# Two graph-attention layers on one core: adjacency loaded by GpSimd's indirect DMA in pieces of 1 MB, edge masks kept with one bit per edge

## The chip, the cores and the metric

The kernel runs on one core of one Trainium2 chip. The metric is the device time of one execution in microseconds. A core has TensorE (PE in the rows; PEld is its weight load), VectorE (DVE), ScalarE (ACT), GpSimd (POOL), the queue engine SyncE (SP), and 16 DMA engines that all queues share.

## What is computed

8192 nodes with 128 features go through two layers of masked attention over the same dense 8192 x 8192 int32 adjacency matrix (268 MB):

```
def layer(x, adj, W, b, a1, a2):
    h  = relu(layernorm(x))
    Wh = h @ W + b
    e  = leaky_relu((Wh @ a1)[:, None] + (Wh @ a2)[None, :], 0.2)   # one score per edge
    p  = softmax(where(adj > 0, e, -9e15), axis=1)
    return x + p @ Wh
x = layer(x, adj, ...)     # layer 0
x = layer(x, adj, ...)     # layer 1, the same adj, other weights
```

## The kernel before

**Scores as signs.** An edge's leaky score is linear in each of its two signs, so the kernel needs for each edge only one bit "edge" and one bit "the score is negative". For each tile of 128 output rows it builds two byte masks, `g1` and `g2`, whose bytes are 0 or one fp8 number, and TensorE multiplies both with prepared node rows (`node_rows`): 128 matmuls for one tile, 64 tiles in a layer. Two `masks` buffers, two `sign_a` and two `sign_z` buffers are used in turn (`T.p` is the tile's parity).

**The stages.** First a node stage computes layer 0's projected rows for 64 node tiles: statistics on VectorE, `rstd` and sums on GpSimd, projection on TensorE, scaled rows on ScalarE, stored to DRAM by SP and loaded back in four quadrants (`load_quadrant`). Then come the 64 tiles of layer 0, then the opening of layer 1, then its 64 tiles.

**Layer 0, tile k.** The bodies of the engines run side by side, each engine in its own written order:
- SP loads 4 MB of adjacency per tile. `adj_sb` has four slots `r` of 1 MB; slot `r` is loaded by four DMAs of 32 partitions x 8 KB (`load_adj`, L248 to L253), and is refilled for the next tile when ScalarE's cast of this tile has read it (`cast_done`, L331). Behind the 16 loads SP stores the finished rows of x, loads x of the next tile and stores the node rows of layer 1.
- ScalarE in body k (L663 to L682): `part_one(k-1)`, at odd k `store_pair`, then cast(k+2, 0), `node_copy(k-2)`, z_sign(k+2, 0), cast(k+2, 1), z_sign(k+2, 1), cast(k+2, 2), `node_high(k-2)`, cast(k+2, 3). A cast turns one adjacency slot to a byte per edge in `sign_a`. `node_high` writes `b_and_d` and then `row_parts`.
- VectorE in body k (L996 to L1039): its two z signs of tile k+1 around the weighing of tile k-1, `mask_bits(k+1)`, `pack(k+1)`, the transpose `turn_bits(k+1)`, `node_ext(k-2)`, the shifts `split_g1` and `split_g2`, and the small steps of tiles k-1 and k-2 between them. `node_low` waits for ScalarE's and GpSimd's `row_parts`.
- `pack` gathers the edge bits of two tiles in the single buffer `pair_a` (1 MB); ScalarE's queue stores it to `mask_dram` after every second tile, and the next even `pack` waits for that store (`pair_stored`, L832).
- GpSimd in body k of layer 1's node work: `node_step(k)` (waits for `var_eps`, which VectorE writes at the end of its body k+1) and `node_rest(k)`, which waits for `ext(k)` and for `b_and_d(k)` of ScalarE's body k+2, and writes half of `row_parts`.
- TensorE in tile k waits for `g_ready(k)` and for the two accumulators of tile k-2. After chunk 8 of 64 it transposes a node tile of layer 1, after chunk 24 it projects it.

**Layer 1.** No adjacency is read: SP loads `pair_a` from `mask_dram` once for two tiles, and VectorE takes each tile's bits from it (`LOW_Z_WORD`, `SHIFT_G1`, `SHIFT_G2` say where the bits lie).

Of the kernel before, what the change touches and what calls it, by code (L numbers as in the profile page):

```python
# [23 lines left out]
NODES = 8192  # L24
# [28 lines left out]
LOW_Z_WORD = [0x10101010, 0x02020202]  # L53
SHIFT_G1 = [0, 3]
SHIFT_G2 = [1, 4]
KEEP_WORD = [0x30303030, 0x06060606]
# [35 lines left out]
def sweep(eng, body, trail=0, step=2, head=HEAD):  # L92

    end = TILES - step
    for k in range(head):
        body(Tile(k))
    with eng.Fori(head // step, end // step) as u:
        for k in range(step):
            body(Tile(k, u, step))
    for k in range(end, TILES + trail):  # L100
        body(Tile(k))


def gat_kernel(nc, x, adj, w_0, b_w_0, a_vec_0, b_a_0, w_1, b_w_1, a_1, out):
# [5 lines left out]
    mask_dram = nc.dram_tensor("mask_bytes", (TILES // 2, 128, NODES), I8, kind="Internal").ap()  # L110
# [4 lines left out]
    with ExitStack() as ctx:  # L115
# [10 lines left out]
        adj_sb = sb("adj_sb", [128, RGROUPS, SPAN], I32)  # L126
        sign_a = sb("sign_a", [128, 2, NODES], I8)
# [119 lines left out]
        def _(sp):  # L247
            def load_adj(T, r):  # L248
                for a in QUAD_ORDER:
                    sp.nop(nofuse=True)  # L250
                    sp.dma_start(adj_sb[QROWS * a:QROWS * (a + 1), r, :],  # L251
                                 adj[ds(T.t * TILE + QROWS * r, QROWS), SPAN * a:SPAN * (a + 1)]) \
                      .then_inc(adj_loaded[r], 16)  # L253

# [48 lines left out]
            adj_after = [BLOCKS, 2 * BLOCKS, 2 * BLOCKS + 3, 3 * BLOCKS]  # L303
            for a in range(QUADS):
                for k in range(BLOCKS * a, BLOCKS * a + NODE_STEP):
# [3 lines left out]
                    if k in adj_after:  # L309
                        load_adj(Tile(0), adj_after.index(k))  # L310
# [11 lines left out]
            def load_pair(T):  # L322
# [3 lines left out]
                sp.dma_start(pair_a[:], mask_dram[ds(T.n, 1), :, :].rearrange("o p c -> p (o c)")).then_inc(pair_loaded, 16)  # L326
# [28 lines left out]
            sp.wait_ge(pair_stored, 16 * TILES // 2)  # L355
# [28 lines left out]
            with sp.Fori(HEAD // 2, TAIL // 2) as u:  # L384
                for k in range(2):
                    layer_1_tile(Tile(k, u))
# [9 lines left out]
        def _(pool):  # L396
# [18 lines left out]
            build_picks()  # L415
            nat_v = nat[:].rearrange("p (c t) -> p c t", c=2)
# [31 lines left out]
            for l in range(LAYERS):  # L448
                if l:
                    pool.wait_ge(S[0].nat_ps, 1)  # L450
                    pool.wait_ge(S[0].coefs, 2)
                    pool.wait_ge(limits, n_limits)

                def body(T):
                    if l and T.u is None and T.k == TILES - 2:
                        pool.wait_ge(S[0].turned, TILES)
                        build_picks()
                    if T.exists:
# [5 lines left out]
                sweep(pool, body, trail=1 - l, step=[NODE_STEP, 2][l])  # L464
# [106 lines left out]
        def _(act):  # L571
# [22 lines left out]
            def cast(T, r):  # L594
# [4 lines left out]
                act.wait_ge(adj_loaded[r], 16 * QUADS * (T.t + 1))  # L599
# [3 lines left out]
            def store_pair(T):  # L603
# [3 lines left out]
                act.dma_start(mask_dram[ds(T.n, 1), :, :].rearrange("o p c -> p (o c)"), pair_a[:]).then_inc(pair_stored, 16)  # L607
# [55 lines left out]
            def layer_0_tile(T):  # L663
# [3 lines left out]
                if T.p == 1 and T.exists and (T.u is not None or T.k < TILES):  # L667
# [16 lines left out]
            sweep(act, layer_0_tile, trail=2)  # L684
# [20 lines left out]
        def _(dve):  # L705
# [107 lines left out]
            def mask_bits(l, T):  # L813
# [4 lines left out]
                else:  # L818
                    dve.wait_ge(pair_loaded, 16 * (T.n + 1))
# [4 lines left out]
                nc.vector.scalar_tensor_tensor(out=bits, in0=bits, scalar=LOW_Z_WORD[T.p], in1=edges,  # L824
# [425 lines left out]
```

## Time and profile before

| | |
|---|---|
| median of 3 runs | 2251.49 us (2243.89 to 2266.31) |
| the profiled execution | 2266.05 us, its span 2264.2 us |
| stages of the span | nodes 0 to 160 us, layer 0 to 1310, opening of layer 1 to 1336, layer 1 to 2264 |
| busy over the span | PE 2015.0 us (89%), PEld 1710.1, DVE 1664.7 (74%), ACT 1134.8 (50%), POOL 347.0 (15%) |
| DMA | 391 MB; 331.62 MB read from HBM, 58.85 MB written |

Busy shares are averages over stages; which engine is late in one of them is read from the waits and the timeline of that stage. A row of the timeline gives start, duration, engine, line and operation, and in brackets the idle time before it with the work that ended it. "SPq" and "ACTq" rows are the issue of a DMA, not its transfer.

### The profile page before, as it was taken

How to read it: one execution, taken by the hardware profiler on the slowest of the kernel's cores; microseconds unless marked ns; L12 is line 12 of the kernel's file. 1: busy time of each engine (PE TensorE's matmuls, PEld its weight loads, DVE VectorE, ACT ScalarE, POOL GpSimd, SP SyncE). 2: the span in 40 equal slices, each digit the busy share in tenths (PEclk: the TensorE clock that was granted, in tenths of full speed). 3: DMA queues.
4: the chain of work that ended last, by engine and by line, in shares of the span. 5: the costliest groups of instructions: out<-in, count | busy, mean ns of one | idle time of the engine just before them, and what ended most of it. 6: DMA issues, size and time to landing. Idle time of an engine off the chain costs nothing.

```text
span 2264.2 us, 49373 instructions
## 1 busy us (share of the span) xinstructions
PE 2015.0 (89%) x16866; PEld 1710.1 (76%) x16866; DVE 1664.7 (74%) x2685; ACT 1134.8 (50%) x1097; POOL 347.0 (15%) x496
## 2 busy tenths in 40 slices
PE   5455889889998898988988979999999999999998
PEld 3234677777777777777877868888888888888887
DVE  6564778778878777787787767777777777777774
ACT  4455667777767676676777433322222223333331
POOL 6440122212222222222222210000000000000000
PEclk9997899999999999999999989999999999999999
DMA  5659999999999999999999681111111111111110
GB/s 145 161 141 243 254 292 280 288 294 309 309 304 269 282 277 278 286 273 288 282 285 296 180 189 47 46 46 46 46 46 46 46 46 46 46 46 46 45 45 11
DMA packets 121683, 390.99 MB, mean 173 GB/s; under 512 B 25137, under 2 KB 74545, under 8 KB 80689
## 3 DMA queue, kind: packets, MB, share of 16 engines
q1 hardware_dynamic: 117040, 357.01, 58.2%
q10 hardware_dynamic: 4608, 33.56, 3.7%
q8 instruction: 18, 0.29, 0.1%
q14 instruction: 17, 0.13, 0.0%
HBM read 331.62 MB, written 58.85 MB: 172 GB/s over the span
## 4 chain that ended last, share of the span: by engine, by line
PE 59%; DMA 25%; DVE 5%; issue 4%; ACT 3%; SPq 2%; DVEq 0%; ACTq 0%; POOL 0%; POOLq 0%
PE acc L538 58%; DMA adj_sb<-in_adj_dram 12%; DMA mask_bytes<-pair_a 11%; DVE masks L845 2%; DMA node_rows<-row_parts 2%; ACT sign_a L600 2%; SPq L251 1%; DVE ext L790 1%; ACT part_a L619 1%; PE ps_h L490 0%; ACT b_and_d L586 0%; ACT row_parts L588 0%; DMA masks<-in_x_dram 0%; DVE row_parts L797 0%; SPq L277 0%
## 5 line engine op out<-in xcount | busy, mean ns | idle before, releaser
L538 PE MATMUL acc<-node_rows,masks 128*128 128x258 f16 x16384 | 1907.9, 278 | 133.7 <-ACT part_a L619 76.0
L538 PEld LDWEIGHTS acc<-node_rows,masks 128*128 128x128 fp8e4 x16384 | 1624.3, 99 | 396.6 <-issue 142.1
L600 ACT ACTIVATE sign_a<-adj_sb 128x2048 int8<-128x2048 int32 x256 | 487.4, 1904 | 142.3 <-DMA adj_sb<-in_adj_dram 137.7
L613 ACT ACTIVATE sign_z<-t_row,neg_s 128x2048 int8<-128x2048 f32 x256 | 503.9, 1994 | 1.0 <-DVE masks L845 1.0
L619 ACT ACTIVATE part_a<-acc,coef_a 128x258 f32<-128x258 f32 x128 | 60.1, 470 | 721.4 <-PE acc L538 721.4
L809 DVE TENSOR_SCALAR sign_z<-t_row,neg_s 128x2048 int8<-128x2048 f32 x256 | 327.0, 1279 | 7.4 <-issue 6.8
L845 DVE STREAM_TRANSPOSE masks<-sign_z 128x2048 uint32<-128x2048 uint32 x128 | 295.0, 2305 | 0.1
L869 DVE SCALAR_TENSOR_TENSOR part_ac<-acc,coef_c,part_a 128x258 f32<-128x258 f32 x128 | 62.1, 485 | 297.8 <-ACT part_a L619 297.6
L435 POOL TENSOR_TENSOR h_sum<-h_sum,ext 128x128 f32<-128x128 f32 x126 | 113.1, 898 | 795.5 <-DVE ext L790 791.8
L833 DVE TENSOR_SCALAR pair_a<-sign_a 128x2048 uint32<-128x2048 uint32 x32 | 39.3, 1227 | 179.8 <-DMA mask_bytes<-pair_a 179.8
L824 DVE SCALAR_TENSOR_TENSOR sign_z<-sign_z,sign_a 128x2048 uint32<-128x2048 uint32 x64 | 146.3, 2285 | 19.7 <-ACT sign_z L613 19.7
L853 DVE TENSOR_SCALAR masks<-masks 128x2048 uint32<-128x2048 uint32 x128 | 155.9, 1218 | 0.1
L860 DVE TENSOR_SCALAR masks<-masks 128x2048 uint32<-128x2048 uint32 x128 | 155.8, 1217 | 0.1
L824 DVE SCALAR_TENSOR_TENSOR sign_z<-sign_z,pair_a 128x2048 uint32<-128x2048 uint32 x64 | 146.3, 2286 | 1.4 <-ACT sign_z L613 1.3
L423 POOL TENSOR_TENSOR rstd<-var_eps,minus_half 128x1 f32<-128x1 f32 x128 | 125.3, 980 | 139.8 <-DVE var_eps L726 139.5
L490 PE MATMUL ps_h<-w_ext,centred_t 128*128 128x133 f32 x256 | 78.0, 397 | 73.1 <-ACT centred_t L575 69.5
L490 PEld LDWEIGHTS ps_h<-w_ext,centred_t 128*128 128x128 f32 x256 | 51.9, 253 | 94.0 <-ACT centred_t L575 71.8
L797 DVE SCALAR_TENSOR_TENSOR row_parts<-ext,b_and_d,row_parts 128x129 f16<-128x129 f32 x256 | 89.0, 349 | 44.6 <-ACT row_parts L588 44.2
L586 ACT ACTIVATE b_and_d<-ext 128x2 f32<-128x2 f32 x128 | 25.6, 200 | 179.3 <-DVE ext L790 132.0
L445 POOL TENSOR_SCALAR row_parts<-ext,b_and_d 128x129 f16<-128x129 f32 x64 | 75.3, 1176 | 17.3 <-ACT b_and_d L586 17.2
L836 DVE SCALAR_TENSOR_TENSOR pair_a<-sign_a,pair_a 128x2048 uint32<-128x2048 uint32 x32 | 73.0, 2282 | 0.0
L485 PE MATMUL ps_t<-ident,centred 128*128 128x128 f32 x128 | 49.4, 388 | 19.6 <-DVE centred L723 18.4
(81 smaller groups left out, 580.2 us busy)
## 6 DMA issues: line engine op xcount, KB each, us to landing
adj_sb<-in_adj_dram SPq DMA_DIRECT2D x1024, 256.0 KB, 10.4
mask_bytes<-pair_a ACTq DMA_DIRECT2D x32, 1024.0 KB, 10.8
pair_a<-mask_bytes SPq DMA_DIRECT2D x32, 1024.0 KB, 4.8
node_rows<-row_parts SPq DMA_DIRECT2D x128, 129.0 KB, 8.1
node_rows<-node_rows SPq DMA_DIRECT2D x32, 516.0 KB, 12.3
x_old<-in_x_dram SPq DMA_DIRECT2D x64, 64.0 KB, 11.9
x_after_layer<-x_new SPq DMA_DIRECT2D x64, 64.0 KB, 12.3
x_old<-x_after_layer SPq DMA_DIRECT2D x64, 64.0 KB, 1.8
```

Source lines behind the costliest of these rows:

```text
L423: pool.tensor_tensor(rstd[:, T.p, :], var_eps[:, T.p, :], minus_half[:], ALU.pow).then_inc(S[l].rstd, 1)
L435: pool.tensor_tensor(h_sum[:], h_sum[:], ext[:, T.p, 0:DIM], ALU.add).then_inc(S[l].h_sum, 1)
L490: pe.matmul(ps_h[:, 0:EXT], centred_t[:, T.p, :], w_ext[l][:], start=True, stop=True).then_inc(S[l].h_raw, 1)
L538: mm = pe.matmul(acc[T.p][s][:, 0:ROW], stationary[s][:, c // BYTES, c % BYTES, :], node_rows[:, c, ROW * s:ROW * (s + 1)], start=(c == 0) ...
L600: nc.scalar.activation(sign_a[:, T.p, SPAN * r:SPAN * (r + 1)], adj_sb[:, r, :], ACT.Sign, scale=-1.0) \
L613: nc.scalar.activation(sign_z[:, T.p, SPAN * r:SPAN * (r + 1)], t_row[:], ACT.Sign, scale=-1.0, bias=neg_s[:, ds(RGROUPS * T.t + r, 1)]).t ...
L797: ins = nc.vector.scalar_tensor_tensor(out=row_parts[:, slot, ROW * s + PART:ROW * (s + 1)], in0=ext[:, T.p, 0:PART], scalar=b_and_d[:, T. ...
L809: nc.vector.tensor_scalar(sign_z[:, T.p, SPAN * r:SPAN * (r + 1)], t_row[:], neg_s[:, ds(RGROUPS * T.t + r, 1)], -1.0, ALU.is_gt, ALU.mult) \
L824: nc.vector.scalar_tensor_tensor(out=bits, in0=bits, scalar=LOW_Z_WORD[T.p], in1=edges, op0=ALU.bitwise_xor, op1=ALU.bitwise_and).then_inc ...
L845: nc.vector.transpose(g2[:, T.p, :].bitcast(U32).rearrange("p (b r i) -> p r b i", r=RGROUPS, i=QROWS), sign_z[:, T.p, :].bitcast(U32).rea ...
L853: nc.vector.tensor_scalar(g1[:, T.p, :].bitcast(U32), words, SHIFT_G1[T.p], EDGE_WORD, ALU.logical_shift_left, ALU.bitwise_and).then_inc(S ...
L860: nc.vector.tensor_scalar(words, words, SHIFT_G2[T.p], EDGE_WORD, ALU.logical_shift_left, ALU.bitwise_and).then_inc(S[l].g_ready, 1)
```

## The change

Three things are changed.

1. The adjacency is loaded by GpSimd. One indirect DMA fills one slot, 128 partitions x 8 KB; partition 32a+i gets columns 2048a to 2048a+2047 of row 128t+32r+i, so one DMA reads 1 MB that is contiguous in DRAM. The row numbers lie in `adj_index` (two sets, each moved on by two tiles after use). Tile 0 is loaded from the fourth step of the first node stage on, tile 1 when its slots are cast, tiles 2 and 3 ahead of layer 1's node work, and then `load_adj(k+4)` stands at the head of GpSimd's body k, ahead of `node_step(k)` and `node_rest(k)`. SP's loads and their place in its order are gone.
2. `pair_a` holds one bit per edge of four tiles. `pack` runs for every tile as before, with other masks (the first of four a tensor_scalar, the other three a scalar_tensor_tensor), the store goes out after every fourth tile, the load in layer 1 comes before every fourth.
3. In layer 1 each tile's bit is doubled in place by VectorE (`double_edges`): one pass ahead of the first of four tiles, two ahead of the last.

```diff
+            def load_adj(T):
+
+                pool.wait_ge(index_ready, QUADS + T.t)
+                for r in range(RGROUPS):
+                    if T.u is not None or T.k:
+                        pool.wait_ge(cast_done, RGROUPS * (T.t - 1) + r + 1)
+                    pool.nop(nofuse=True)
+                    pool.indirect_dma_start(out=adj_sb[:, r, :], out_offset=None, in_=adj_rows_of_2048,
+                                            in_offset=bass.IndirectOffsetOnAxis(ap=adj_index[:, T.p, r:r + 1], axis=0)) \
+                        .then_inc(adj_loaded[r], 16)
+                if T.u is None and T.k == 0:
+                    pool.engine_nop().then_inc(index_ready, 1)
+                else:
+                    pool.tensor_scalar(adj_index[:, 1 - T.p, :], adj_index[:, 1 - T.p, :], float(2 * QUADS * TILE), 1.0,
+                                       ALU.add, ALU.mult).then_inc(index_ready, 1)
...
             for l in range(LAYERS):
                 if l:
+                    load_adj(Tile(1))
                     pool.wait_ge(S[0].nat_ps, 1)
                     pool.wait_ge(S[0].coefs, 2)
                     pool.wait_ge(limits, n_limits)
+                    for k in range(2, LOADS_AHEAD):
+                        load_adj(Tile(k))
...
+                    if l == 0 and T.u is None and T.k == HEAD - 1:
+                        load_adj(Tile(0))
+                    if l and T.plus(LOADS_AHEAD).exists:
+                        load_adj(T.plus(LOADS_AHEAD))
                     if T.exists:
                         node_step(l, T)
                     rest = T.plus(l - 1)
                     if rest.exists:
                         node_rest(l, rest)
...
-                act.wait_ge(adj_loaded[r], 16 * QUADS * (T.t + 1))
+                act.wait_ge(adj_loaded[r], 16 * (T.t + 1))
...
-                if T.p == 1 and T.exists and (T.u is not None or T.k < TILES):
+                if T.p4 == PACK - 1 and (T.u is not None or T.k < TILES):
                     store_pair(T)
...
             def layer_0_tile(T):
-                if T.plus(1).exists:
-                    for r in range(RGROUPS):
-                        sp.wait_ge(cast_done, RGROUPS * T.t + r + 1)
-                        load_adj(T.plus(1), r)
...
-                if T.p == 1 and T.plus(1).exists:
+                if T.p4 == PACK - 1 and T.plus(1).exists:
                     load_pair(T.plus(1))
...
+            def double_edges(T):
+
+                pair = pair_a[:].bitcast(U32)
+                if T.p4 == 0:
+                    dve.wait_ge(pair_loaded, 16 * (T.n4 + 1))
+                    dve.nop(nofuse=True)
+                    nc.vector.scalar_tensor_tensor(out=pair, in0=pair, scalar=1, in1=pair, op0=ALU.logical_shift_right,
+                                                   op1=ALU.bitwise_or).then_inc(edges_ready, 1)
+                if T.p4 == PACK - 1:
+                    dve.wait_ge(S[1].edge_bits, T.t)
+                    nc.vector.tensor_scalar(pair, pair, LAST_BIT_UP, LAST_BIT_WORD, ALU.logical_shift_left, ALU.bitwise_and) \
+                        .then_inc(edges_ready, 1)
+                    dve.wait_ge(edges_ready, 3 * T.n4 + 2)
+                    dve.nop(nofuse=True)
+                    nc.vector.scalar_tensor_tensor(out=pair, in0=pair, scalar=1, in1=pair, op0=ALU.logical_shift_right,
+                                                   op1=ALU.bitwise_or).then_inc(edges_ready, 1)
...
-                if T.p == 0:
+                if T.p4 == 0:
                     if T.u is not None or T.k:
-                        dve.wait_ge(pair_stored, 16 * T.n)
+                        dve.wait_ge(pair_stored, 16 * T.n4)
                     nc.vector.tensor_scalar(pair, edges, KEEP_WORD[0], None, ALU.bitwise_and).then_inc(packed, 1)
```

## Rows read from the trace of the kernel before

**Rows 1.** Windows by stage: length, busy (count) per engine, clock, DMA share, GB/s

```profile
0.00:160.00 160.00, 84.22 (x223) 50.16 (x224) 98.38 (x482) 75.03 (x263) 88.05 (x220) 1.00 0.58 146
160.00:1310.00 1150.00, 1002.07 (x8403) 849.81 (x8401) 874.45 (x1331) 783.92 (x633) 256.36 (x269) 0.94 1.00 277
...
1336.00:2264.00 928.00, 918.40 (x8192) 800.92 (x8192) 674.02 (x832) 262.65 (x187) 0.00 (x0) 0.99 0.14 46
```

**Rows 2.** Waits in 500:1290: engine, line, releaser, us in total, times, longest

```profile
DVE pair_a L833 <- DMA mask_bytes<-pair_a: 141.4, 23, 7.6
...
PE acc L538 <- ACT part_a L619: 76.0, 21, 4.8
...
ACT sign_a L600 <- DMA adj_sb<-in_adj_dram: 30.5, 33, 2.0
```

**Rows 3.** Timelines of ACT, DVE and PE from one mask store on

```profile
912.97 0.34 ACTq L607 DMA_DIRECT2D mask_bytes<-pair_a  x1
...
924.14 1.23 DVE L833 TENSOR_SCALAR pair_a<-sign_a 128x2048 uint32<-128x2048 uint32 x1 [6.60 <-DMA mask_bytes<-pair_a]
...
929.68 1.21 DVE L860 TENSOR_SCALAR masks<-masks 128x2048 uint32<-128x2048 uint32 x1
...
931.14 3.45 PE L538 MATMUL acc<-node_rows,masks 128*128 128x258 f16 x18 [3.86 <-ACT part_a L619]
```

**Rows 4.** The chain that ended last: mask stores of bodies 17 and 61

```profile
495.95 10.21 DMA mask_bytes<-pair_a
...
1260.92 10.38 DMA mask_bytes<-pair_a
```

**Rows 5.** Timelines of PE and ACT: first tiles, tiles 2 and 63 weighed

```profile
176.64 15.84 PE L538 MATMUL acc<-node_rows,masks 128*128 128x258 f16 x128 [12.85 <-DVE masks L860]
206.51 16.24 PE L538 MATMUL acc<-node_rows,masks 128*128 128x258 f16 x128 [14.03 <-DVE masks L860]
...
249.77 0.46 ACT L619 ACTIVATE part_a<-acc,coef_a 128x258 f32<-128x258 f32 x1
...
1309.38 0.47 ACT L619 ACTIVATE part_a<-acc,coef_a 128x258 f32<-128x258 f32 x1 [7.69 <-PE acc L538]
```

**Rows 6.** Timeline of ACT: casts 0 and 2 of body 50, a b_and_d

```profile
907.77 0.20 ACT L586 ACTIVATE b_and_d<-ext 128x2 f32<-128x2 f32 x1
...
913.48 1.91 ACT L600 ACTIVATE sign_a<-adj_sb 128x2048 int8<-128x2048 int32 x1 [0.24 <-issue]
...
921.04 1.90 ACT L600 ACTIVATE sign_a<-adj_sb 128x2048 int8<-128x2048 int32 x1
```

**Rows 7.** Timelines: POOL beside a busy and an idle DVE, and that DVE

```profile
909.23 1.35 POOL L445 TENSOR_SCALAR row_parts<-ext,b_and_d 128x129 f16<-128x129 f32 x1
911.57 1.43 POOL L423 TENSOR_TENSOR rstd<-var_eps,minus_half 128x1 f32<-128x1 f32 x1 [0.98 <-DVE var_eps L726]
...
911.32 1.27 DVE L809 TENSOR_SCALAR sign_z<-t_row,neg_s 128x2048 int8<-128x2048 f32 x1
...
1301.85 0.47 POOL L445 TENSOR_SCALAR row_parts<-ext,b_and_d 128x129 f16<-128x129 f32 x1
...
1307.08 0.55 POOL L423 TENSOR_TENSOR rstd<-var_eps,minus_half 128x1 f32<-128x1 f32 x1
```

**Rows 8.** DMA issues: queue, count, KB each, median us from issue to landing

```profile
adj_sb<-in_adj_dram SPq DMA_DIRECT2D x1024, 256.0 KB, 10.4
mask_bytes<-pair_a ACTq DMA_DIRECT2D x32, 1024.0 KB, 10.8
pair_a<-mask_bytes SPq DMA_DIRECT2D x32, 1024.0 KB, 4.8
```

**Rows 9.** Windows: one pair_a load of layer 1, alone on the DMA engines

```profile
1515.20:1520.00 4.80, 4.80 (x46) 4.18 (x44) 4.80 (x7) 0.00 (x0) 0.00 (x0) 1.00 0.60 218
```

**Rows 10.** Waits in 1336:2264, and the groups of pack and mask_bits

```profile
DVE part_ac L869 <- ACT part_a L619: 244.4, 64, 12.4
...
L833 DVE TENSOR_SCALAR pair_a<-sign_a 128x2048 uint32<-128x2048 uint32 x32 | 39.3, 1227 | 179.8 <-DMA mask_bytes<-pair_a 179.8
L836 DVE SCALAR_TENSOR_TENSOR pair_a<-sign_a,pair_a 128x2048 uint32<-128x2048 uint32 x32 | 73.0, 2282 | 0.0
```

**Rows 11.** Node stage: chain that ended last, and SP's timeline

```profile
22.64 8.20 DMA masks<-in_x_dram
...
91.75 15.59 DMA node_rows<-row_parts
...
87.63 1.82 SPq L251 DMA_DIRECT2D adj_sb<-in_adj_dram  x4
```

**Rows 12.** Timeline of DVE at the opening of layer 1

```profile
1328.92 2.29 DVE L824 SCALAR_TENSOR_TENSOR sign_z<-sign_z,pair_a 128x2048 uint32<-128x2048 uint32 x1 [1.30 <-ACT sign_z L613]
```

More of the change, by code:

```diff
@@ L50 @@
 EDGE_WORD = 0x20202020
[L53 to L56, printed above, removed]
+PACK = 4
+KEEP_WORD = [0x80808080, 0x20202020, 0x08080808, 0x02020202]
+LAST_BIT_UP, LAST_BIT_WORD = 5, 0x40404040
+LOW_Z_WORD = [[0x10101010, 0x02020202] * 2, [0x40404040, 0x10101010, 0x04040404, 0x20202020]]
+LEFT_G1 = [[0, 3] * 2, [-2, 0, 2, -1]]
+LEFT_G2 = [[1, 4] * 2, [-1, 1, 3, 0]]
 VGROUPS = 4
@@ L89, in wait_before, with sweep @@
             eng.wait_ge(sem, self.t - back + 1)
-def sweep(eng, body, trail=0, step=2, head=HEAD):
-    end = TILES - step
+def sweep(eng, body, trail=0, step=2, head=HEAD, tail=None):
+    end = TILES - (tail or step)
     for k in range(head):
@@ L247, in _ @@
         def _(sp):
[L248 to L253, printed above, removed]
             def load_x_old(l, T):
@@ L383, in _ @@
                 layer_1_tile(Tile(k))
-            with sp.Fori(HEAD // 2, TAIL // 2) as u:
-                for k in range(2):
-                    layer_1_tile(Tile(k, u))
+            with sp.Fori(HEAD // PACK, TAIL // PACK) as u:
+                for k in range(PACK):
+                    layer_1_tile(Tile(k, u, PACK))
             for k in range(TAIL, TILES):
@@ L415, in _ @@
             build_picks()
+            pool.iota(adj_index[:].rearrange("p b r -> p (b r)"), pattern=[[QUADS * TILE, 2], [QUADS * QROWS, RGROUPS]], base=0,
+                      channel_multiplier=QUADS).then_inc(index_ready, 1)
+            pool.wait_ge(index_ready, 1)
+            for a in range(1, QUADS):
+                part = adj_index[QROWS * a:QROWS * (a + 1), :, :].rearrange("p b r -> p (b r)")
+                pool.tensor_scalar(part, part, float(a - QUADS * QROWS * a), 1.0, ALU.add, ALU.mult).then_inc(index_ready, 1)
+                pool.wait_ge(index_ready, a + 1)
+            adj_rows_of_2048 = adj.rearrange("n (a c) -> (n a) c", a=QUADS)
+            def load_adj(T):
[12 more added lines that the diff above has]
+                                       ALU.add, ALU.mult).then_inc(index_ready, 1)
             nat_v = nat[:].rearrange("p (c t) -> p c t", c=2)
@@ L462, in body @@
                         node_rest(l, rest)
-                sweep(pool, body, trail=1 - l, step=[NODE_STEP, 2][l])
+                sweep(pool, body, trail=1 - l, step=[NODE_STEP, 2][l], tail=[NODE_STEP, LOADS_AHEAD][l])
         @block.tensor
@@ L682, in layer_0_tile @@
                     cast(ahead, 3)
-            sweep(act, layer_0_tile, trail=2)
+            sweep(act, layer_0_tile, trail=2, step=PACK)
             open_layer(1)
@@ L835, in pack @@
                     dve.wait_ge(packed, T.t)
-                    nc.vector.scalar_tensor_tensor(out=pair, in0=edges, scalar=KEEP_WORD[1], in1=pair,
+                    nc.vector.scalar_tensor_tensor(out=pair, in0=edges, scalar=KEEP_WORD[T.p4], in1=pair,
                                                    op0=ALU.bitwise_and, op1=ALU.bitwise_or).then_inc(packed, 1)
@@ L847, in turn_bits, with to_edge_bit @@
                   .then_inc(S[l].turned, 1)
+            def to_edge_bit(out, words, left):
+                shift = ALU.logical_shift_left if left >= 0 else ALU.logical_shift_right
+                return nc.vector.tensor_scalar(out, words, abs(left), EDGE_WORD, shift, ALU.bitwise_and)
             def split_g1(l, T):
@@ L1008, in tile @@
                     if ahead.exists:
+                        if l:
+                            double_edges(ahead)
                         mask_bits(l, ahead)
@@ L1043, in _ @@
                     choose_path()
-                sweep(dve, tile, trail=2 - l)
+                sweep(dve, tile, trail=2 - l, step=PACK)
         fast_path.close()
```

29 lines of the change are left out of this document (13 added, 16 removed).

## The prediction

> **What bounds the kernel now.** I read the windows by stage first: layer 0 takes 1150 of 2264 us, with the DMA engines busy all the time (share 1.00) at 277 GB/s, while layer 1 is TensorE alone (918.40 us busy of 928) with DMA at 0.14 [rows 1]. So the change can win only in layer 0 and the node stage ahead of it. Then the waits of layer 0's steady part, where the largest on the path is VectorE's even `pack` waiting for the mask store, 141.4 us in 23 times, and TensorE's that follow from it, 76.0 us in 21; ScalarE's casts hardly wait for the adjacency, 30.5 us [rows 2]. The timeline shows the loop that this makes. The store is issued at 912.97 and landed when `pack` starts at 924.14; transpose and shifts end at 930.89, and TensorE starts its tile at 931.14 after 3.86 us of idling, its first 18 matmuls in 3.45 us, 192 ns each where layer 1 takes 918.40/8192 = 112 ns [rows 1, 3]. With the tile's end comes the next store. 22 such rounds of two tiles fill 495.95 to 1260.92, so a tile costs 17.39 us [rows 4], where TensorE needs 128 x 0.112 = 14.35 us and some 0.3 for the node matmuls: 14.65. The first tiles are worse: tile 1 starts at 206.51, 14.03 us late for its masks, and tile 2 is weighed at 249.77 [rows 5]. From there to the weighing of tile 63 at 1309.38 are 61 tiles of 17.37 us.
>
> **The mask store every fourth tile.** The wait of 6.60 us [rows 3] comes half as often. If nothing else were late, four tiles would cost 4 x 14.65 + 3.86 + 18 x 0.08 = 63.9 us, 16.0 a tile.
>
> **The loads' rate.** A 1 MB load over 128 partitions keeps the engines busy 0.60 x 4.80 = 2.88 us, which is 364 GB/s [rows 9]; the 32-partition loads fill them at 277 [rows 1]. The Trainium skill, page "SBUF — State Buffer", section "Door 1: The DMA port swizzle", says that 32 partitions reach 8 of 16 ports and only 128 reach all; the two rates agree with its direction. A tile moves 4.19 MB of adjacency, 0.26 of masks, 0.26 of x and node rows, together 4.7: 13.0 us at 364 GB/s, 17.0 at 277. I take the first, since these loads have its shape; the second is a rival.
>
> **Where the loads are issued, and what they wait for.** This is where I expect the gain to be spent. SP could refill a slot as soon as its cast was done. GpSimd's body k starts with the loads of tile k+4, but it comes there only after `node_rest(k-1)`, which waits for `b_and_d(k-1)`; ScalarE writes that in body k+1, behind casts 0, 1 and 2 of tile k+3. So slots 0 to 2 stand empty until then, and slot 0 is needed again at the head of ScalarE's next body. A ring is closed once per tile, and its length is a sum:
> - from cast 0 to the end of cast 2, with the copy and both z signs: 921.04 + 1.90 - 913.48 = 9.4 us; then `b_and_d`, 0.2 us [rows 6];
> - GpSimd's `row_parts`: 0.47 us beside an idle VectorE, 1.35 beside a busy one [rows 7]. VectorE's `node_low` waits for this very operation in this ring, so I take 0.5;
> - writing the descriptors of one indirect DMA: no row has it. From below SP's issues, 1.82/4 = 0.45 us [rows 11]; from above GpSimd's worst stretching: `rstd` takes 0.55 us alone and 1.43 when it meets VectorE's 1.27 us tensor_scalar, which it sits out [rows 7], so 1 us of work behind two z signs would be 3.5 us. It stands right ahead of z sign 2 of the next body: one meeting, 1.6 us taken;
> - landing: 4.8 us on a quiet queue, 10.8 for a 1 MB transfer among others [rows 8]. Four loads follow one another and need 3 x 2.9 us behind the first, so the queue is nearly empty when the next ring comes round: 4.8 taken.
>
> Sum 9.4 + 0.2 + 0.5 + 1.6 + 4.8 = 16.5 us. In every fourth body the mask store leaves just as load 0 does and shares the engines with it, 2.9 us at most: 0.4 a tile on average. 16.9 us. VectorE's own wait for that store then lies beside the ring: the store lands some 9 us after issue, and `ext` comes about when ScalarE reaches `b_and_d` anyway.
>
> So a tile would cost 16.9 where it cost 17.37, and TensorE would idle about 2 us in each tile, at chunk 24, because its projection waits for `node_copy`, which follows cast 0. The ring is above the 16.0 us of the store alone, so 16.9 is the period.
>
> **The start of layer 0.** Tile 0 starts when it did (176.64) and tile 1 right behind it, at 192.5: the loads of tile 1 go out as tile 0 is cast, ahead of that point as before, and arrive 1 MB every 2.9 us, and tiles 2 and 3 are loaded ahead of the node work. Tile 2 is weighed at 192.5 + 2 x 15.5 = 223.5, 26 us earlier than at 249.77 [rows 5]. Then 59 tiles of 16.9 and two without loads at 14.9 give 1250.4 for tile 63, against 1309.38: 59 us gained, 26 of them before the steady part and 33 in it.
>
> **The rest.** Node stage: row stores wait up to 15.59 us behind quadrant and adjacency loads on SP's ring [rows 11]; 1 MB less in three of these is 3 x 2.9, about 9 us gained. Against that, 4 MB of adjacency now go out early, beside the x loads, for which VectorE already waits 8.20 us [rows 11]: up to 4.19/0.364 = 11.5 us, 7 taken, and 4 x 1.6 us of descriptors on a GpSimd that is in the step's loop. Together 4 us lost (9 gained to 18 lost). Opening of layer 1: one more pass of 2.28 us on VectorE, of which 1.30 fits in its wait [rows 12], 1 us. Layer 1: VectorE's waits are 244.4/64 = 3.8 us a tile, and the added passes are 2.28 us for one tile of four and 1.23 + 2.28 = 3.5 for another [rows 10]. They fit, with 0.3 us to spare; without that cover the second would cost at most 16 x 1 us. 1 us taken. The pack's third and fourth pass of 2.28 where one was 1.23 add 0.26 us a tile to a VectorE that is not the ring. The pair loads halve.
>
> Sum: 2266.05 - 59 + 4 + 1 + 1 = 2213 us for the profiled execution; scaled to the median of the runs (2251.49/2266.05) 2199, say 2200.
>
> **The rivals.**
> - *The loads are fast enough* (descriptors and landing together under 5.5 us). Then the mask store's 16.0 us is the period. For it: the quiet-queue 4.8 us contains an issue already. Against: GpSimd's instructions are 2.6 to 2.9 times as long beside VectorE. 53 us less than my forecast: 2147.
> - *No more bandwidth.* The indirect loads get 277 GB/s; 17.0 us of transfers a tile, the queue never drains, load 0 lands behind the last ones, about 17.7 us. For it: the reads come from the same DRAM rows, and the layer-1 load had the chip to itself. 59 x 0.8 = 47 us more: 2247, no difference.
> - *GpSimd is starved* (slower). While VectorE runs its passes GpSimd writes no descriptors. If each of the four waits for one or two passes, issue takes 3.5 us and load 0 lands at 5.5, `row_parts` back at 1.35: 9.4 + 0.2 + 1.35 + 3.5 + 5.5 + 0.4 = 20.4 us a tile, 59 x 3.5 = 206 more: 2405. The gain is gone from a period of 17.9 us on, which is descriptors and landing at 7.4 instead of 6.4 us, so a milder form of it, 18.4 us, already ends at 2288. The Trainium skill states this mechanism outright: page "SBUF — State Buffer", section "Summary: rules for kernel authors", advises the hardware queues because descriptor writing starves while VectorE is in its faster modes. The rows support the stretching of GpSimd's arithmetic [rows 7]; no run so far shows a descriptor.
>
> **How the numbers follow.** Chances: my ring 0.45, fast loads 0.20, no more bandwidth 0.15, starved 0.20 (most of it mild). A measurement of this kernel tells 1% from no change, 22 us. Faster by over 1%: 0.45 x 0.85 + 0.20 + 0.15 x 0.3 = 0.63; slower by over 1%: 0.16 of the starved and 0.03 of the third; 0.18 between. The range runs from 2125 (below the fast loads, with the node stage's best end) to 2300 (mild starvation).
>
> **What would show it.** Right: casts waiting for `adj_sb` some 4 to 5 us once per tile (250 us and more over layer 0, where its steady part had 30.5), nearly all at cast 0; TensorE idling at the projection for ScalarE's copy rather than at the tile's head; `pack` waiting in only 15 places; tile 2 weighed near 224; layer 1 at 918 us. Wrong: cast 0 not waiting (the order of GpSimd's body costs nothing), GpSimd's DMA instructions far from 1 to 2 us, a DMA share still at 1.00 in layer 0, or a node stage that is longer by more than 20 us.

## The result, and the profile after

The change made the kernel slower by 0.9%: 2271.29 us median of 11 runs (2267.00 to 2274.79) against 2247.78 us of 11 (2236.70 to 2266.31), a ratio of 1.0092 [1.0066, 1.0118]. The forecast was 2200.

| us | before | after | forecast |
|---|---|---|---|
| profiled execution | 2266.05 | 2267.00 | 2213 |
| tile 2 of layer 0 weighed | 249.77 | 222.61 | 223.5 |
| a tile of the steady part (tiles 2 to 60) | 17.43 | 17.92 | 16.9 |
| tile 63 weighed | 1309.38 | 1308.21 | 1250.4 |
| from there to the end of the span | 954.8 | 956.9 | 956.8 |

The head start of 27 us was won, and 59 tiles at half a microsecond more each took it away again. The page of the changed kernel, its busy line and the row of the casts:

```profile
PE 2016.6 (89%) x16866; PEld 1708.1 (75%) x16866; DVE 1778.2 (79%) x2733; ACT 1123.6 (50%) x1097; POOL 762.0 (34%) x819
...
L622 ACT ACTIVATE sign_a<-adj_sb 128x2048 int8<-128x2048 int32 x256 | 486.1, 1900 | 305.0 <-DMA adj_sb<-in_adj_dram,adj_index 300.7
```

The windows by stage, for comparison with [rows 1]:

```profile
0.00:160.00 160.00, 85.15 (x226) 50.69 (x227) 98.08 (x482) 75.43 (x263) 96.71 (x233) 1.00 0.55 150
160.00:1310.00 1150.00, 1002.09 (x8402) 849.15 (x8401) 898.02 (x1334) 772.34 (x633) 662.74 (x580) 0.95 0.71 262
1336.00:2264.00 928.00, 919.70 (x8188) 799.57 (x8186) 761.89 (x873) 261.25 (x187) 0.00 (x0) 0.99 0.09 28
```

TensorE does the same in the same 1150 us of layer 0, but the DMA engines that were full (share 1.00) are now free for 29% of it, while 262 GB/s went through where 277 did. So the traffic as a whole moves at 262/0.71 = 369 GB/s of busy time: the engines have time left, and the loads are issued too late. The same stretch of waits as in [rows 2] says where:

```profile
ACT sign_a L622 <- DMA adj_sb<-in_adj_dram,adj_index: 220.6, 45, 7.8
POOL row_parts L460 <- ACT b_and_d L608: 155.4, 44, 5.1
DVE row_parts L819 <- ACT row_parts L610: 109.0, 43, 4.1
PE ps_h L512 <- ACT centred_t L597: 97.4, 40, 5.5
```

ScalarE waits for the adjacency once per tile, 4.9 us, where all its waits of that kind were 30.5 us; GpSimd waits once per tile for ScalarE; TensorE stops at its projection, not at the head of a tile. The wait of `pack` for the mask store is nearly gone (141.4 us before). The four together are one ring, and two turns of it can be read off the timelines. ScalarE from cast 0 of one body on (start, duration, idle time before with its releaser):

```profile
911.78 1.91 ACT L622 ACTIVATE sign_a<-adj_sb 128x2048 int8<-128x2048 int32 x1 [5.55 <-DMA adj_sb<-in_adj_dram,adj_index]
...
919.34 1.90 ACT L622 ACTIVATE sign_a<-adj_sb 128x2048 int8<-128x2048 int32 x1
921.14 0.19 ACT L608 ACTIVATE b_and_d<-ext 128x2 f32<-128x2 f32 x1
...
928.74 1.91 ACT L622 ACTIVATE sign_a<-adj_sb 128x2048 int8<-128x2048 int32 x1 [3.68 <-DMA adj_sb<-in_adj_dram,adj_index]
...
938.11 0.20 ACT L608 ACTIVATE b_and_d<-ext 128x2 f32<-128x2 f32 x1
...
940.47 0.34 ACTq L629 DMA_DIRECT2D mask_bytes<-pair_a  x1
947.91 1.91 ACT L622 ACTIVATE sign_a<-adj_sb 128x2048 int8<-128x2048 int32 x1 [7.01 <-DMA adj_sb<-in_adj_dram,adj_index]
```

GpSimd beside it:

```profile
921.53 0.38 POOL L460 TENSOR_SCALAR row_parts<-ext,b_and_d 128x129 f16<-128x129 f32 x1 [4.37 <-ACT b_and_d L608]
922.65 1.41 POOL L422 DMA_INDIRECT adj_sb<-in_adj_dram,adj_index  x1 [0.73 <-issue]
924.37 0.94 POOL L422 DMA_INDIRECT adj_sb<-in_adj_dram,adj_index  x1 [0.31 <-issue]
...
938.56 0.38 POOL L460 TENSOR_SCALAR row_parts<-ext,b_and_d 128x129 f16<-128x129 f32 x1 [2.51 <-ACT b_and_d L608]
939.44 1.59 POOL L422 DMA_INDIRECT adj_sb<-in_adj_dram,adj_index  x1 [0.50 <-issue]
...
943.14 3.61 POOL L422 DMA_INDIRECT adj_sb<-in_adj_dram,adj_index  x1 [0.30 <-issue]
```

First turn: cast 0 at 911.78, cast 2 done at 921.24, `row_parts` 921.53 to 921.91, first descriptors written at 922.65 + 1.41 = 924.06, landed 4.68 later at 928.74: 16.96 us. Second turn: descriptors done at 941.03, but the mask store left at 940.47 and the load lands 6.88 us later: 19.17 us. The mean of 36 turns between 500 and 1200 us, beside the forecast's terms:

| term, us | forecast | measured |
|---|---|---|
| cast 0 to `b_and_d`, which starts 0.1 before the end of cast 2 | 9.4 | 9.38 |
| start of `b_and_d` to the start of `row_parts` | 0.2 | 0.42 |
| `row_parts` | 0.5 | 0.38 |
| end of `row_parts` to the first indirect DMA | not counted | 0.62 |
| its descriptors | 1.6 | 1.57 |
| end of descriptors to cast 0 | 4.8 | 4.97 in the three bodies without a store |
| mask store, shared over four | 0.4 | 0.52 (7.04 in the body with the store) |
| sum | 16.9 | 17.86 |

The ring was found, but taken 0.96 us too short; over 59 tiles that is 57 us of the 57.8 by which tile 63 came later than forecast. What the store does in the ring is seen in the packets of the trace: the first packet of load 0 moves 0.70 us after the end of its descriptors in the bodies without a store, and 3.40 us after it in the nine bodies with one, about when the store's last packets end (0.56 us before, on average). So load 0 stands behind the store more than it shares the engines with it.

TensorE's stop of 4.18 us at the projection is followed by a lower granted clock. PE's timeline, then windows of the same stretch (the clock is the third number from the end), and VectorE's `pack` of that body:

```profile
950.02 0.49 PE L512 MATMUL ps_h<-w_ext,centred_t 128*128 128x133 f32 x2 [4.18 <-ACT centred_t L597]
950.36 12.54 PE L560 MATMUL acc<-node_rows,masks 128*128 128x258 f16 x96
```

```profile
946.00:950.00 4.00, 0.00 (x0) 0.00 (x0) 3.18 (x4) 2.09 (x3) 2.45 (x4) 1.00 1.01 428
950.00:951.50 1.50, 1.48 (x10) 1.22 (x11) 0.94 (x3) 1.50 (x1) 0.42 (x1) 0.78 1.00 426
951.50:953.00 1.50, 1.50 (x9) 1.05 (x8) 1.50 (x3) 1.50 (x2) 1.07 (x2) 0.50 1.04 437
953.00:955.00 2.00, 2.00 (x14) 1.53 (x13) 0.86 (x2) 2.00 (x2) 0.00 (x0) 0.68 0.92 365
955.00:963.00 8.00, 8.00 (x74) 7.00 (x73) 3.50 (x8) 5.14 (x6) 3.99 (x4) 1.00 0.29 87
```

```profile
945.40 1.23 DVE L872 TENSOR_SCALAR pair_a<-sign_a 128x2048 uint32<-128x2048 uint32 x1 [0.22 <-DMA mask_bytes<-pair_a]
```

0.50 is the 1.2 GHz level. The 96 matmuls took 12.54 us; at layer 1's 919.70/8188 = 0.112 us each they take 10.8. No term of the ring above has TensorE in it, and ScalarE reached `b_and_d` in these turns without waiting for `ext`, so the slower matmuls lie beside the ring here. The last row says that the mask store had landed by 945.40; by the packets of the trace, what the DMA engines move from 946 to 953 are the queued indirect loads alone (428, 426 and 437 GB/s).

### The profile page after: what moved, and what is told of

Same layout as the page of the kernel before. It is cut to its first block, busy times and chain, and to the rows that moved or that the text cites. A ratio compares the mean times of both kernels' runs of the same rounds, so it can differ in the third digit from the quotient of the medians.

```text
span 2265.1 us, 46517 instructions
## 1 busy us (share of the span) xinstructions
PE 2016.6 (89%) x16866; PEld 1708.1 (75%) x16866; DVE 1778.2 (79%) x2733; ACT 1123.6 (50%) x1097; POOL 762.0 (34%) x819
## 4 chain that ended last, share of the span: by engine, by line
PE 47%; DMA 19%; ACT 14%; issue 14%; DVE 3%; POOL 1%; POOLq 0%; SPq 0%; DVEq 0%; ACTq 0%
PE acc L560 46%; DMA adj_sb<-in_adj_dram,adj_index 17%; ACT sign_a L622 8%; ACT sign_z L635 4%; DMA node_rows<-row_parts 2%; POOL adj_sb L422 1%; DMA masks<-in_x_dram 1%; ACT centred_t L597 1%; DVE ext L812 1%; PE ps_h L512 1%; PE acc L529 0%; ACT b_and_d L608 0%; DVE sign_z L846 0%; DVE masks L884 0%; ACT row_parts L610 0%
## 5 line engine op out<-in xcount | busy, mean ns | idle before, releaser
L422 POOL DMA_INDIRECT adj_sb<-in_adj_dram,adj_index x256 | 447.3, 1747 | 121.6 <-issue 94.6
L512 PE MATMUL ps_h<-w_ext,centred_t 128*128 128x133 f32 x256 | 85.8, 430 | 180.1 <-ACT centred_t L597 172.7
L875 DVE SCALAR_TENSOR_TENSOR pair_a<-sign_a,pair_a 128x2048 uint32<-128x2048 uint32 x48 | 109.5, 2282 | 0.0
L460 POOL TENSOR_SCALAR row_parts<-ext,b_and_d 128x129 f16<-128x129 f32 x64 | 26.4, 412 | 211.4 <-ACT b_and_d L608 211.4
L438 POOL TENSOR_TENSOR rstd<-var_eps,minus_half 128x1 f32<-128x1 f32 x128 | 92.8, 726 | 10.1 <-DVE var_eps L748 4.8
L812 DVE SCALAR_TENSOR_TENSOR ext<-ps_h,rstd,bias 128x133 f32<-128x133 f32 x128 | 43.0, 336 | 36.5 <-PE ps_h L512 35.8
## 6 DMA issues: line engine op xcount, KB each, us to landing
node_rows<-node_rows SPq DMA_DIRECT2D x32, 516.0 KB, 11.7
```

What stands on the lines that cost most here:

```text
L422: pool.indirect_dma_start(out=adj_sb[:, r, :], out_offset=None, in_=adj_rows_of_2048, in_offset=bass.IndirectOffsetOnAxis(ap=adj_index[:, ...
L438: pool.tensor_tensor(rstd[:, T.p, :], var_eps[:, T.p, :], minus_half[:], ALU.pow).then_inc(S[l].rstd, 1)
L512: pe.matmul(ps_h[:, 0:EXT], centred_t[:, T.p, :], w_ext[l][:], start=True, stop=True).then_inc(S[l].h_raw, 1)
L875: nc.vector.scalar_tensor_tensor(out=pair, in0=edges, scalar=KEEP_WORD[T.p4], in1=pair, op0=ALU.bitwise_and, op1=ALU.bitwise_or).then_inc( ...
```

## The experiments

Ten kernels, each an edit of the changed one unless said. The period is that of tiles 2 to 60. Each ratio is to the kernel before on the same chip, whose median there lay between 2247.78 and 2255.42, so ratios are compared, and medians only for large steps. The periods and rows are those of one profiled execution each; that of e3 is the fastest of its four (2188.19 of 2188.19 to 2223.25), so its median belongs to a longer period than the one shown.

| run | what | median | ratio to before [95%] | period |
|---|---|---|---|---|
| changed kernel | | 2271.29 | 1.0092 [1.0066, 1.0118] | 17.92 |
| e1 | loads spread over GpSimd's body | 2165.58 | 0.9628 [0.9588, 0.9668] | 16.09 |
| e3 | packing alone, SP loads | 2211.91 | 0.9849 [0.9786, 0.9912] | 16.19 |
| e4 | loads alone, two tiles per byte | 2300.35 | 1.0223 [1.0181, 1.0266] | 18.35 |
| e5 | store a little earlier | 2264.53 | 1.0055 [1.0033, 1.0076] | 17.88 |
| e6 | ring lengthened | 2312.03 | 1.0238 [1.0156, 1.0321] | 18.56 |
| e7 | `b_and_d` earlier | 2243.00 | 0.9951 [0.9913, 0.9990] | 17.57 |
| e8 | `row_parts` ahead of the sums, loads spread | 2130.96 | 0.9442 [0.9357, 0.9527] | 15.52 |
| e9 | e8 with two tiles per byte | 2196.99 | 0.9728 [0.9649, 0.9808] | 16.60 |
| e10 | e8 with the store earlier | 2077.09 | 0.9216 [0.9193, 0.9239] | 14.65 |
| e11 | store earlier still | 2247.75 | 0.9954 [0.9927, 0.9981] | 17.61 |

**e1: is it the order of GpSimd's body?** Only the places of the four loads move; each of them, with its `cast_done` wait, stays.

```diff
             def node_rest(l, T):
+                ahead = T.plus(LOADS_AHEAD + 1)
+                if l and ahead.exists:
+                    load_adj(ahead, (0,))
                 pool.wait_ge(S[l].ext, T.t + 1)
...
+                if ahead.exists:
+                    load_adj(ahead, (1, 2))
                 pool.wait_ge(S[l].b_and_d, T.t + 1)
...
                                    ALU.mult, ALU.mult).then_inc(S[l].high_d, 1)
+                if ahead.exists:
+                    load_adj(ahead, (3,))
```

> The changed kernel with GpSimd's order alone altered: the load of slot 0 of tile k+5 ahead of node_rest(k), slots 1 and 2 ahead of its wait for b_and_d, slot 3 behind row_parts. Ring theory: slots are refilled as they are cast, as on SP before; the ring of 17.9 us per tile is opened and the period falls to 16.0 us or a little above (mask store every fourth tile, TensorE's 14.65 otherwise): about 110 us less than the changed kernel, near 2160. Rival, descriptors starved or DMA rate the limit: order is without effect, 2270. A further rival, GpSimd now holds up h_sum and rstd behind loads that wait for casts: between 2200 and 2270.

Measured: 2165.58 us, period 16.09, 106 us below the changed kernel with the same loads, bytes and passes. Windows and waits of 500:1100:

```profile
500.00:1100.00 600.00, 558.48 (x4883) 474.44 (x4881) 520.85 (x783) 463.75 (x376) 393.51 (x338) 1.00 0.78 293
```

```profile
POOL h_sum L456 <- DVE ext L822: 168.1, 37, 6.7
DVE row_parts L829 <- POOL row_parts L468: 78.3, 38, 3.2
...
ACT sign_a L632 <- DMA adj_sb<-in_adj_dram,adj_index: 21.1, 15, 2.4
```

The casts wait 21.1 us where they waited 175.0 in this stretch. So the ring through `b_and_d` set the period. In its place VectorE now waits for GpSimd's `row_parts`, 2.1 us in 38 tiles: the sums and the loads of slots 1 and 2 stand ahead of it.

**e3 and e4: the two halves alone.** e3 keeps the four-tile masks and puts SP's loads back; e4 keeps GpSimd's loads and packs two tiles.

```diff
+            def load_adj(T, r):
+                for a in QUAD_ORDER:
+                    sp.nop(nofuse=True)
+                    sp.dma_start(adj_sb[QROWS * a:QROWS * (a + 1), r, :],
+                                 adj[ds(T.t * TILE + QROWS * r, QROWS), SPAN * a:SPAN * (a + 1)]) \
+                      .then_inc(adj_loaded[r], 16)
...
             def layer_0_tile(T):
+                if T.plus(1).exists:
+                    for r in range(RGROUPS):
+                        sp.wait_ge(cast_done, RGROUPS * T.t + r + 1)
+                        load_adj(T.plus(1), r)
```

```diff
-KEEP_WORD = [0x80808080, 0x20202020, 0x08080808, 0x02020202]
+KEEP_WORD = [0x30303030, 0x06060606]
...
-                if T.p4 == PACK - 1 and (T.u is not None or T.k < TILES):
+                if T.p == 1 and T.exists and (T.u is not None or T.k < TILES):
                     store_pair(T)
...
-            def double_edges(T):
```

> One half of the change: four tiles per byte, the adjacency loaded by SP as before. If the store's wait was the period before (17.4 us), it falls to 16.0 to 16.7 us a tile, 40 to 70 us less: 2180 to 2210. Rival, the DMA engines at share 1.00 were the limit as well: 0.26 MB of 5 MB less a tile, 0.9 us at most, 17.0 or more: 2225 or above, as the store's wait turns into casts that wait for adj_sb.

> The other half: adjacency by GpSimd, two tiles per byte as before. Ring theory: the ring of 17.3 us stays, and load 0 shares the engines with a mask store in every second body instead of every fourth (2.1 us each time): 18.4 us a tile, 30 us more than the changed kernel: 2300. Rival, the mask store does not matter to the loads: 2270.

Measured: 2211.91 and 2300.35 us. Packing alone gains 1.5%, the loads alone cost 2.2%, and the two nearly add up to the 0.9% of both. e3's median came out just above what was expected for it and below its rival's 2225. Windows and waits of 500:1100 in its fastest execution:

```profile
500.00:1100.00 600.00, 553.64 (x4842) 476.67 (x4840) 510.31 (x772) 454.98 (x370) 141.03 (x148) 0.99 1.03 291
```

```profile
ACT sign_a L605 <- DMA adj_sb<-in_adj_dram: 111.9, 83, 2.7
DVE pair_a L855 <- DMA mask_bytes<-pair_a: 48.7, 10, 6.3
```

With fewer store waits the 32-partition loads become late themselves: 83 short waits of the casts at a DMA share of 1.03 and 291 GB/s. By that rate a tile's 4.7 MB take 16.2 us, the period of this execution (an estimate from these rows), so loads of this shape leave little below it. In e4 the store falls on the ring every second tile; from its issue to cast 0:

```profile
815.48 0.34 ACTq L626 DMA_DIRECT2D mask_bytes<-pair_a  x1
822.95 1.91 ACT L619 ACTIVATE sign_a<-adj_sb 128x2048 int8<-128x2048 int32 x1 [7.06 <-DMA adj_sb<-in_adj_dram,adj_index]
```

Bodies with a store take 19.3 us there and the others 17.35, so the store costs the ring 2 us each time. One store less in four tiles is 0.5 us a tile or some 30 us in 59 tiles, which covers what packing still buys in the changed kernel: 2300 to 2271.

**e5 and e11: the store off the ring.** e5 issues it in the body before, behind `node_high`; e11 behind cast 1 of that body.

```diff
-                if T.p4 == PACK - 1 and (T.u is not None or T.k < TILES):
-                    store_pair(T)
...
                     cast(ahead, 1)
+                if T.p4 == PACK - 2 and (T.u is not None or T.k < TILES):
+                    store_pair(T.plus(1))
+                if ahead.exists:
                     z_sign(0, ahead, 1)
                     cast(ahead, 2)
```

> The changed kernel with the mask store issued 2.3 us earlier, ahead of cast 3 of the body before instead of behind part_one. Ring theory: load 0 of that tile (8.6 us from issue to cast against 6.5) loses most of its delay, 1 to 2 us in four tiles, 15 to 30 us in all: 2240 to 2255. Rival, the longer landing in the fourth tile comes from elsewhere (the even pack, descriptors held up): 2270.

> The changed kernel with the mask store issued behind cast 1 of the body before, when the loads of that body have mostly landed, so that it has landed before load 0 of the next tile is issued. Ring theory with a term for sharing: load 0 of the fourth tile falls from 8.6 to 6.5 us, four tiles by 2.1 us, 31 us in all: near 2240. Rival, that body's longer landing comes from something else in it: above 2260.

e5: 2264.53, missed; by its timeline the issue of the store began only 1.0 us, and ended 0.6 us, ahead of load 0's descriptors, and load 0 still took 8.34 us from issue to cast, so it told nothing on its own. e11: 2247.75, near what was expected; in its fourth bodies that time is 7.11 us, where it was 8.64, and 6.59 to 6.75 in the others. The store's term is worth 23.5 us by the medians (0.31 x 59 = 18 by the period, 0.0138 x 2250 = 31 by the ratios), of at most 0.52 x 59 = 31.

**e6: the same ring, lengthened on purpose.** Two GpSimd additions of 0.5 us ahead of the loads of every tile.

```diff
+                for k in range(2):
+                    pool.tensor_tensor(scratch[:], ident[:], ident[:], ALU.add).then_inc(index_ready, 1)
+                    pool.wait_ge(index_ready, QUADS + 3 * T.t + k + 1)
```

> The changed kernel with two additions of 128x128 on GpSimd (0.55 us each alone) ahead of the first load of every tile. Ring theory: they lie between row_parts and the descriptors of load 0, so each of some 59 periods is longer by what they take, 1.1 us alone and up to 2.6 beside VectorE: 65 to 150 us more, 2335 to 2420. Rival, the period is set by DMA bandwidth or by VectorE, with GpSimd idle for two thirds of the time: 2270 as before.

Measured: 2312.03, +41 us by the medians (33 by the ratios), the period +0.64. The sign is the theory's and the case without a ring is out, but the size is below what the theory expected. GpSimd's timeline shows the additions in place:

```profile
836.53 0.38 POOL L464 TENSOR_SCALAR row_parts<-ext,b_and_d 128x129 f16<-128x129 f32 x1 [4.77 <-ACT b_and_d L612]
836.87 1.01 POOL L420 TENSOR_TENSOR scratch<-ident 128x128 f32<-128x128 f32 x2
838.77 1.40 POOL L426 DMA_INDIRECT adj_sb<-in_adj_dram,adj_index  x1 [0.89 <-ACT sign_a L626]
```

From `row_parts` to the first load it is now 1.83 us, 1.21 more; the descriptors of load 0 take 1.77 us where they took 1.57, and the landing is shorter, 4.72 us on average where it was 5.49. 1.21 + 0.20 - 0.77 is the 0.64. A later load meets less of the store: the landing falls from 7.04 to 5.23 us in the bodies with one. It also falls from 4.97 to 4.56 us in the others, and why is open. So landing was no constant of the ring, and the expectation, which held it fixed, came out too large.

**e7: `b_and_d` one cast earlier.** Its `node_high` goes behind cast 1, which takes 3.9 us (a z sign and a cast) out of the ring.

```diff
                     cast(ahead, 1)
-                    z_sign(0, ahead, 1)
-                    cast(ahead, 2)
                 if before.exists:
                     node_high(1, before)
                 if ahead.exists:
+                    z_sign(0, ahead, 1)
+                    cast(ahead, 2)
+                if ahead.exists:
                     cast(ahead, 3)
```

> The changed kernel with ScalarE's node_high behind cast 1 instead of behind cast 2; GpSimd's order stays. Ring theory: a z sign and a cast, 3.7 us, leave the ring of 17.9 us, and another limit takes over (about 16.1, as in the interleaved version): about 2165 to 2180. Rival, what the interleaved version gained came from issuing the loads spread out in time rather than from the ring: 2250 or above.

Measured: 2243.00, a third of the gain expected, and below the 2250 of the rival. GpSimd now stands behind `ext` instead (164.7 us in 500:1100, 66.4 before the edit), and works beside a busy VectorE. GpSimd's rows, then two of VectorE in the same turn:

```profile
817.29 1.34 POOL L450 TENSOR_TENSOR h_sum<-h_sum,ext 128x128 f32<-128x128 f32 x1 [2.53 <-DVE ext L813]
818.57 0.25 POOL L451 COPY nat<-ext 128x2 f32 x1
818.81 1.35 POOL L460 TENSOR_SCALAR row_parts<-ext,b_and_d 128x129 f16<-128x129 f32 x1
820.33 1.95 POOL L422 DMA_INDIRECT adj_sb<-in_adj_dram,adj_index  x1 [0.17 <-issue]
```

```profile
807.97 0.49 DVE L912 SCALAR_TENSOR_TENSOR part_ac<-acc,coef_c,part_a 128x258 f32<-128x258 f32 x1 [1.42 <-ACT part_a L641]
...
816.80 0.32 DVE L813 SCALAR_TENSOR_TENSOR ext<-ps_h,rstd,bias 128x133 f32<-128x133 f32 x1
```

So right behind the first path lay a second, whose end is `ext`, `h_sum`, `row_parts`, load 0, with `h_sum` and `row_parts` at 1.35 us each. It does not come straight from the projection: none of the 34 `ext` of this stretch waits for it (it had ended 1.6 to 8.7 us before). `ext` is late by VectorE's own order, in which a z sign, `mask_bits`, `pack` and the transpose stand ahead of it. The last thing that VectorE had waited for (by over 0.3 us) before an `ext` was ScalarE's `part_a`, hence the end of a tile on TensorE, in 25 tiles, and the mask store in the other 9 (47.6 us). TensorE's slower matmuls after a stop can therefore lie on this path, though they lay beside the first. The forecast had not listed it.

**e8 and e9: both rings opened.** Loads 0 and 1 ahead of the wait for `ext`, then `row_parts`, load 2, the sums, load 3; e9 is the same with two tiles per byte, as in e4.

```diff
             def node_rest(l, T):
-                pool.wait_ge(S[l].ext, T.t + 1)
+                ahead = T.plus(LOADS_AHEAD + 1)
+                if l and ahead.exists:
+                    load_adj(ahead, (0, 1))
+                pool.wait_ge(S[l].ext, T.t + 1)
...
+                if ahead.exists:
+                    load_adj(ahead, (2,))
+                keep_sums(l, T)
+                if ahead.exists:
+                    load_adj(ahead, (3,))
```

> The interleaved version with GpSimd's row_parts moved ahead of the sums and behind loads 0 and 1 (there VectorE waited 2.04 us a tile for it, with h_sum and two DMA issues in front of it). If that wait is the period's 1.4 us over TensorE's 14.65, the period falls from 16.1 to about 14.9: some 65 us less, near 2100. Rival, the next limit is close behind (DMA at 0.78 busy, landing of load 1 behind the mask store): 2130 to 2165.

> The version before this one with two tiles per byte as in the kernel before. If the mask store only mattered through DMA engines that the 32-partition loads kept full, the packing is now worth next to nothing (0.26 MB a tile, 0.7 us of DMA time that is free, against 0.26 us of VectorE): within 15 us of it. Rival, each store holds up a load by 2 us and the tile with it, in every second tile instead of every fourth: 20 to 30 us slower.

Measured: 2130.96 and 2196.99, both above what was expected: e8 lies at the edge of its rival's range, though with the mask store's wait and not a late load behind it, and e9 lies outside both of its cases. Waits of e8 in 500:1100:

```profile
DVE pair_a L887 <- DMA mask_bytes<-pair_a: 48.3, 9, 5.6
...
PE acc L575 <- ACT part_a L656: 23.7, 9, 2.9
```

The casts no longer wait, and the store's wait of the kernel before has become the bound again, in half as many places; e9 has it twice as often (90.0 us in 17). With the loads' ring out of the way the packing is worth 66 us, where in the changed kernel it is worth 29.

**e10: and the store earlier.** e8 with the store issued one body ahead, in front of `node_high`.

```diff
                     cast(ahead, 2)
+                if T.p4 == PACK - 2 and (T.u is not None or T.k < TILES):
+                    store_pair(T.plus(1))
                 if before.exists:
                     node_high(1, before)
```

> The version with loads interleaved and row_parts first (2131), and the mask store issued ahead of node_high in the body before, as soon as its pack is done. There every fourth even pack waits 5.3 us for a store that lands after 10 us; the store now goes out some 6 us earlier. If that wait is what is left over TensorE's 14.65 us, four tiles fall from 62.1 to about 59 us and layer 0 by 45 us: near 2088. Rival, DMA engines at 0.84 busy: the early store holds up the loads instead and casts wait for them, 2115 or above.

Measured: 2077.09 us, 7.8% below the kernel before. Windows and waits of 500:1100:

```profile
500.00:1100.00 600.00, 600.00 (x5367) 525.61 (x5365) 576.22 (x859) 489.29 (x404) 473.00 (x363) 1.00 0.87 315
```

```profile
ACT part_a L656 <- PE acc L575: 94.9, 41, 2.6
```

TensorE is busy for all 600 us, a tile takes 14.65 us, the figure worked out for TensorE alone, and the other engines wait for it. All three parts of the change are in this kernel; only places in two orders differ. The same early store with SP's loads was not tried.

## Why the prediction was wrong

- *The sign was wrong because a sum was too small.* The step that failed is the sum of the ring, 16.9 us; it came to 17.86. The gap of 0.62 us between `row_parts` and the first indirect DMA had no term, `b_and_d` was taken at its own 0.2 us though its result is used 0.42 us after its start, and the landing came to 5.49 us on average where 5.2 (4.8 + 0.4) was taken: 0.62 + 0.22 + 0.29, less 0.12, 0.03 and 0.02 for `row_parts`, the descriptors and the casts, is 0.96. The margin against the old period was only 0.5 us a tile, and 1.0 with the 26 us of the start; the two uncounted hand-overs add 0.84. I took point values for 7 us of issue and landing of which no row existed, and the "4.8" from a transfer that was alone on its queue. "Shares the engines" was not it either: load 0 stands behind the store, 2.07 us in every fourth body, 0.52 a tile where 0.4 was taken.
- *The mechanism was right.* e1 takes the ring away and gains 106 us, e6 lengthens it and loses 33 to 41, e4 has it without the new packing at 2300. Casts wait some 4.9 us once per tile, TensorE stops at the projection, `pack` hardly waits, tile 2 is weighed at 222.61 (223.5 forecast).
- *The reference point was scaled.* 2213 was made for the profiled execution and multiplied by 2251.49/2266.05. Before's profiled execution was at the top of its runs, 18 us above its median of 11; after's lies 4 below its own. So of the 71 us between 2200 and 2271.29, 54 are 2213 to 2267.00, and 17 are the scaling. It also moved the break-even: against the profiled execution it is a period of 17.9 us, as forecast, but against the median 2247.78 it is 23.5/59 = 0.4 us less, 17.5; between the ratios of e11 (0.9954 at 17.61) and of the changed kernel (1.0092 at 17.92) it would be 17.7. So the traces show why nothing was gained (2267.00 against 2266.05). That the changed kernel's median lies 23.5 us above the other's rests for the most part on the scatter of the kernel before, and no trace was taken of an execution of it near its median. Why its executions spread over 30 us and those of the changed one over 8 is open.
- *Rivals.* "Fast loads" asked for descriptors and landing under 5.5 us together; they take 7.06, or 7.7 with the gap. "No more bandwidth" falls: the share is 0.71, not 1.00, and e10 moves 315 GB/s at 0.87, 362 at a full share, as in [rows 9]. The Trainium skill, page "SBUF — State Buffer", section "Door 1: The DMA port swizzle", says that transfers over 128 partitions reach all 16 ports and those over 32 reach 8; the traces agree in direction, 362 to 369 GB/s of all traffic at a full share, and 426 to 437 for queued loads alone, against 277 to 291. The 128-partition loads also read 1 MB that is contiguous in DRAM, and no run separates the two. "Starved GpSimd": the 256 indirect DMAs take 0.93 us at least, 1.59 in the median and 3.69 at most, the longest beside VectorE's passes. So it exists, at the size that the forecast had in its 1.6, and is not the cause: the same instructions are in e10 at TensorE's own pace. The Trainium skill, page "SBUF — State Buffer", section "Summary: rules for kernel authors", would have such loads on a hardware queue because of it. The trace agrees with the stretching, but it did not keep e10 from TensorE's pace. Whether a hardware queue would do as well is open: e3 with SP's loads ends at 2211.91, but differs from e10 (2077.09) in the loads' shape and in the place of the mask store too, and 128-partition loads on SP were not tried.
- *The other terms.* Node stage: +4 forecast, tile 0 starts at 176.46 us (176.64 before). The x loads wait 14.41 us where they waited 8.20, and the row stores behind the quadrants 11.2 to 11.7 where they had up to 15.59. Both came about in the size forecast (6.2 us lost where 7 were taken, and 43.2 us of the three stores down to 34.3 where 9 gained were taken), but the 6.4 us of descriptors added to them did not show in the total. So the 4 us lost were too many, and hide 4 us of the ring's error in the 54 above. The waits after the change:

```profile
26.81 14.41 DMA masks<-in_x_dram
...
65.66 11.67 DMA node_rows<-row_parts
...
98.25 11.19 DMA node_rows<-row_parts
...
130.37 11.46 DMA node_rows<-row_parts
```

Layer 1: 919.70 us of TensorE against 918.40, VectorE's waits down to 150.1 us from 244.4 [rows 10], as the cover of the added passes said. Tile 63 to the end is 2.1 us longer, 2 forecast.

## What to carry to other kernels

When loads move from a queue of their own into an engine's written order, follow one load round: what it waits for, all that stands before it, issue, landing, use, and back to that wait; add every hand-over (0.2 and 0.6 us here), and if the sum is within a microsecond of the present period, say that the sign is open. Put each refill right behind what frees its slot and ahead of waits that it does not need: the same loads and the same packing are 0.9% slower than the kernel before in one order (the changed kernel) and 7.8% faster in another (e10). After a ring is opened look at once for the next one (`ext` in e7, the mask store in e8), and forecast a change as a difference to a median, not from one profiled execution.

## What the runs showed of the hardware

An indirect DMA of 128 rows of 8 KB occupies GpSimd for 0.93 to 3.69 us, median 1.59; one follows another after 0.30 us. The first behind a `row_parts` of 0.38 us comes 0.50 to 0.75 us after its end, but behind one of 1.35 us only 0.17 after it (e7): counted from the start of `row_parts` that is 0.88 to 1.13 us in the one case and 1.52 in the other, so part of the gap lies beside a longer instruction. How long one takes goes with what VectorE does beside it: the 13 of more than 3 us in the changed kernel all ran beside `mask_bits` (2.28 us) and then `pack`, while 16 of the 55 of at most 1.0 us ran beside VectorE's transpose of 2.3 us, which did not hold them up. Indirect loads that queue behind one another moved 426 to 437 GB/s at a share of about 1.0 (windows above), 1 MB in about 2.45 us, and the first packet of a load moved 0.70 us after its descriptors when no store was ahead of it. TensorE's granted clock was at 0.50 within 2 us after a stop of 4.18 us, and back at 1.00 some 5 us after the stop.
